# A GpSimd wait for landed rows in the middle of each attention step of a graph network kernel

## The reference

```
scores = einsum('ehd,ehd->eh', q[dst], k[src] + ep[:, None, :]) * scale
scores = scores * ew[:, None]
ex     = exp(scores - m[dst])              # m: maximum over the edges of a node
attn   = ex / segment_sum(ex, dst)[dst]
out    = segment_sum(attn[:, :, None] * v[src], dst)
x = x + alpha * (out @ Wo + bo);  x = x + beta * (gelu(norm(x) @ W1 + b1) @ W2 + b2)
```

## Time and profile before

| | |
|---|---|
| time, median of 3 runs | 2524.44 us (2523.85 to 2524.78) |
| span of the profiled execution | 2736.8 us |
| the profiled execution's own time | none is recorded beside its span |
| share of the span: PE, PEld, DVE, ACT, POOL | 77%, 59%, 80%, 56%, 59% |
| mean granted TensorE clock | 0.882 |
| indirect gathers of `kv_e` (L1358) | 752, of 953 ns mean on GpSimd |
| edge lists (L1337) | 94 |

### The profile page before, as it was taken

One profiled execution on the slowest core, in us unless ns is written; L12 is line 12 of the kernel. 1 busy time (PEld: TensorE's weight loads), 2 busy tenths in 40 slices (PEclk: granted clock), 3 DMA queues, 4 the chain that ended last, 5 costly groups with the idle time before them and its releaser, 6 DMA issues. The chain is left out here.

```text
span 2736.8 us, 41806 instructions
## 1 busy us (share of the span) xinstructions
PE 2107.6 (77%) x9647; PEld 1611.0 (59%) x9647; DVE 2183.1 (80%) x3415; ACT 1524.3 (56%) x4291; POOL 1618.3 (59%) x1808
## 2 busy tenths in 40 slices
PE   3999999999999999679815666666566666656666
PEld 2787878777777777533314455455455545545555
DVE  6888888888888888645546878878888788878793
ACT  5787888788877887433223444444444444444443
POOL 5666666666666666342246666666666666666642
PEclk8999999999999999889957788878878878887787
DMA  6232222222222222769856666666666666666651
GB/s 203 72 84 81 83 83 83 83 82 84 83 83 81 84 82 84 167 165 253 234 181 168 168 173 175 173 165 173 177 169 175 169 172 176 167 175 170 173 141 45
DMA packets 157414, 379.08 MB, mean 139 GB/s; under 512 B 47810, under 2 KB 63298, under 8 KB 157186
## 3 DMA queue, kind: packets, MB, share of 16 engines
q0 software_dynamic: 100544, 309.00, 40.6%
q1 hardware_dynamic: 44946, 68.53, 8.7%
q10 hardware_dynamic: 11904, 1.34, 0.4%
HBM read 353.36 MB, written 37.07 MB: 143 GB/s over the span
## 5 line engine op out<-in xcount | busy, mean ns | idle before, releaser
L1358 POOL DMA_INDIRECT kv_e<-kv_rows,edge x752 | 716.9, 953 | 408.4 <-issue 223.4
L487 POOL DMA_INDIRECT feat<-in_x_rows,idx x664 | 677.1, 1020 | 236.2 <-issue 234.8
L523 ACT ACTIVATE vsh<-feat,rec_a 128x256 f32<-128x256 f32 x1980 | 806.8, 495 | 8.9 <-DMA feat<-in_x_rows,idx 4.8
L1541 PE MATMUL ps_sum<-kv_e,ident 128*128 128x264 f32 x1504 | 473.8, 477 | 376.9 <-issue 264.2
L1541 PEld LDWEIGHTS ps_sum<-kv_e,ident 128*128 128x128 f32 x1504 | 352.5, 240 | 481.8 <-issue 283.6
L571 PE MATMUL ps_a<-msg,hot 128*128 128x257 f32 x1312 | 409.4, 393 | 4.0 <-issue 4.0
L573 PE MATMUL ps_a<-msg,hot 128*128 128x256 f32 x1312 | 390.6, 379 | 0.1
L575 PE MATMUL ps_a<-msg,hot 128*128 128x192 f32 x1312 | 320.2, 325 | 0.0
L573 PEld LDWEIGHTS ps_a<-msg,hot 128*128 128x128 f32 x1312 | 248.6, 190 | 38.2 <-issue 1.9
L575 PEld LDWEIGHTS ps_a<-msg,hot 128*128 128x128 f32 x1312 | 248.8, 190 | 34.9
L571 PEld LDWEIGHTS ps_a<-msg,hot 128*128 128x128 f32 x1312 | 222.2, 189 | 66.3 <-issue 66.3
(11 more groups left out here) (419 smaller groups left out, 3182.2 us busy)
## 6 DMA issues: line engine op xcount, KB each, us to landing
ef<-in_ef_t SPq DMA_DIRECT2D x84, 256.0 KB
kv_e<-kv_rows,edge POOLq DMA_INDIRECT x752
rows_e<-rows SPq DMA_DIRECT2D x41, 272.0 KB
feat<-in_x_rows,idx POOLq DMA_INDIRECT x664
rows_e<-in_ef_t SPq DMA_DIRECT2D x1, 7446.0 KB, 26.6
kv_rows<-kv SPq DMA_DIRECT2D x20, 260.0 KB, 2.5
rows_e<-in_ef_t SPq DMA_DIRECT2D x1, 3706.0 KB
x<-x_rows SPq DMA_DIRECT2D x23, 128.0 KB
```

Source lines behind the costliest of these rows:

```text
L487: pool.indirect_dma_start(out=feat[:, u, c, 0, :, :].rearrange("p a b -> p (a b)"), out_offset=None, in_=g.x_rows, in_offset=bass.Indirect ...
L523: ins = act.activation(vsh[:, u % TURN, c, j, :, :], feat[:, u % TURN, c, 0, :, :], ACT.Copy, scale=rec_a[:, u % 2, c, 1 + j:2 + j])
L1358: pool.indirect_dma_start(out=kv[:, u, s, :], out_offset=None, in_=g.kv_rows, in_offset=bass.IndirectOffsetOnAxis(ap=edge[:, u, s, DH + 1: ...
L1541: mm = pe.matmul(out, g.ident[:], kv[:, u, s, D:], start=(s == 0), stop=False, skip_group_check=True)
```

## The change

In the middle of a step, ahead of the edge list of the next step, GpSimd waits until four gathers of this step have landed. `v_kv[u]` has 128 for each of the t rounds before and 16 for each gather of this one, so `t * 128 + 64` is reached when the step's four gathers so far are all in. A semaphore that nobody waits for is raised then. The wait is in all 94 steps, those of the tail too; what is gathered, its order and its buffers stay the same.

```
                 for s in range(SLOTS):
                     if s == SLOTS // 2:
+                        pool.wait_ge(v_kv[u], t * (16 * SLOTS) + 16 * HALF)
+                        pool.sem_inc(v_asked_pool, 1)
                         if more:
                             pool.wait_ge(v_at, k + 2)
                             pool.wait_ge(v_read, k + 1)
```

## The result

| | before | after |
|---|---|---|
| time, median | 2524.14 us (2522.99 to 2524.78, 4 runs) | 2847.9 us (2844.3 to 2848.52, 4 runs) |
| span of the profiled execution | 2736.8 us | 2845.8 us, its own time 2847.47 |
| ratio | | 1.1281, 95% interval 1.1267 to 1.1294 |

Now and then an execution takes over 1.5% longer than the fastest of its kernel (3232.85 us in one case, where most took 2752 to 2768), and medians and ratios in this document are of the others alone.

The account below looks back on a forecast made before the run. The prediction took GpSimd's nine issues a step, 11.33 us, to bound the attention stage, with DVE right behind. Adding 3.4 us for each of 94 waits gave 2524.4 + 319.6 = 2844 us, range 2740 to 2885.

Parts of the forecast that it names:

- The price of the wait: GpSimd's mid-step gap grows from 0.30 us by landing plus restart, adding 3.34 to 3.54 us a step, taken as 3.4.
- landing to DVE's start: From the end of a step's last gather issue to DVE, which waits for it, starting: 2.95 to 2.99 us.
- GpSimd's restart beyond DVE's: Where both engines are let go together, GpSimd's next issue comes 0.67 to 0.87 us behind DVE.
- The 3.0 us made from the Trainium skill's fit: Alternative addition per mid-step wait: 2.6 us for one DMA, plus restart 0.67 less 0.30; total 2806 us.
- The beat as the bound: In the attention stage GpSimd's nine issues, 11.33 us a step, set the pace; the wait makes it 14.73.
- What is covered: The delayed edge list stays hidden behind four gathers, 5.0 us against 3.00 of landing; the added increment costs nothing.
- rival E: TensorE, its clock kept at 1.2 GHz by longer pauses, bounds the attention stage: 2938 us, chance 0.03.
- The step that was right for a wrong reason: Attention-stage stops of up to 12 us were taken as the profiled execution's, mostly absent from timed runs.
- the 2484.7 us worked out for a stage without them: End of the attention stage if GpSimd never waited, 198.7 us earlier than profiled.
- Rival A: Attention-stage stops occur in timed runs too, hiding 2.3 us of each wait: 120.9 us added, 2645 us, chance 0.11.
- The stretch outside the stage: Of the 212.4 us between profiled span and median, the attention stage without waits explained 198.7, within 14 us.
- The span forecast for the profile of after: Profiled span of the changed kernel: 2858 us, with the attention stage ending 120.9 us later than in the first profile.

Follow-up runs that it names:

- the three shorter waits: Kernel before plus a mid-step wait for three gathers, or for two, or for four behind the edge list's issue: 2728.97, 2610.87, 2725.96 us.
- the wait that is already met: Kernel before plus a mid-step wait for the step's edge list, already waited for, with the increment: 2521.82 us, ratio 1.000.
- with seven gathers: Kernel before with SP loading the eighth slot: ratio 0.9672; adding the change's wait 0.9985, or a wait for two gathers 0.9701.
- both waits: Kernel before plus the change's mid-step wait and a wait for all eight gathers at each step's end: 3208.4 us, ratio 1.1622.
- the wait at the end of the step: Kernel before plus a wait for all eight gathers at each step's end, none in the middle: 2878.62 us, ratio 1.0427.
- one wait a lap: Kernel before plus the change's wait in one step of each lap of four: u = 3 2770.62 us, u = 1 2786.02 us.

## Why the prediction was right

*The price of the wait.* Put at 3.34 to 3.54 us, taken as 3.4; measured 323.8 / 94 = 3.44. Both terms, read from engines that waited for something else, held as they were defined: landing to DVE's start 2.95 to 2.99 predicted, 2.91 in the row of after; GpSimd's restart beyond DVE's 0.67 to 0.87 predicted, 0.83 there. By the landings' own updates the same gap is 2.77 and 0.98. The 3.0 us made from the Trainium skill's fit ("DMA: Bandwidth & Descriptors", anatomy of one DMA on the gpsimd path) would have given 2806. Here the measurement decides for the rows.

*The beat as the bound.* Held: 94 times the price lies on top, and the three shorter waits follow it to within 3 us. The sum, 2844, is 3.9 us below the 2847.9 measured.

*What is covered.* Held: the edge list may be late (the wait behind it costs the same as the wait for three gathers), the increment is free (the wait that is already met). Once GpSimd has slack, a wait shorter than the slack is nearly free: with seven gathers, 7 us for 88.8, on a chip where about half of that slack came from the stops (an estimate, above).

*TensorE at its lower level (rival E).* Did not happen: at a clock of 0.78 TensorE was busy 836.84 of 1393 us, and even at a beat above 18 us, with both waits, the second cost what one wait costs.

*The step that was right for a wrong reason.* "I take these as stops that the profiled execution has and the timed ones mostly have not." The timed runs of the result indeed have none, and the 2484.7 us worked out for a stage without them is what this rested on. But they are no mark of a single profiled execution: on three chips out of four in the experiments the timed runs are long too, and the profiled execution of after, on the other side, agrees with its own time to 2 us. The first profile must have come from such a chip, or been taken in the same way; that is inferred from its stops and from the semaphore updates that it lacks, since no time stands beside it. Rival A, "the stops are real in the timed runs too", is thereby the other kind of chip: its price of 120.9 us agrees with what the wait at the end of the step costs there, 119.6. Had the result been timed on such a chip, the ratio would by this have been near 1.04 instead of 1.13, with a time near the 2879 of the wait at the end; that is an estimate, and it was not run. So the price of the wait was foreseen by its mechanism, and its base, a timed program without stops, was worked out. But that the changed kernel would meet the same kind of chip was not argued, since the prediction did not know of two kinds; there it was lucky.

*The stretch outside the stage.* The prediction left 13.7 us of the 212.4 without a place. The profile of the already met wait finds it. Against the first profile of before it is 217.1 us shorter (2519.7 for 2736.8): 195.9 in the stage, where the prediction had 198.7, 13.5 ahead of it (first gather at 1387.59 for 1401.05) and 7.8 behind it (45.6 us for 53.4). The span forecast for the profile of after, 2858, started from that first profile and is 12 us too long, mostly for the same reason: in the 2845.8 measured, the first gather is issued at 1389.94.

Open: why the engines stand on some chips and not on others, whether recording has a part in it, and why they move when the traffic is over. A full wait in every step removes the stops (none in the profiles with the wait at the end, with both, and with seven gathers and the change's wait); a wait for two of seven gathers in every step does not, nor does one wait a lap. I have no run that separates the gathers' traffic from the work of the engines around them.

## What to carry to other kernels

A wait for one's own DMA costs landing plus the issuing engine's restart, less the issues that run in between, here 2.8 + 1.0 - 0.3 us; their sum can be read before the change from other engines' rows. Each issue moved ahead of the wait takes its own length off the price, and a wait as short as the slack is free, so count the slack of the issuing engine first. And where a profile's span and the timed median differ by 8%, don't explain the difference away: sum the engines' own beats, see which of the two they give, and treat the other as a second case with its own price.

## What the runs showed of the hardware

The same program took 2522 us on one chip and 2746, 2759 and 2763 on three others, each figure steady within a per cent. Between the profiles of 2519.7 and 2760.9 us all of the difference lies in one stage but some 22 us (12.6 ahead of it, 8.9 behind it). In the second one DVE stands for "remote" for up to 13.7 us, 29 times and 186.8 us in all in 1220 us of the stage. At the stop that was looked at closely TensorE is recorded in drips, with the parts of one matmul 2.8 us apart, ScalarE stands for 10.1 us with no release shown, and a semaphore update of TensorE comes 12.6 us behind the recorded end of its matmul. The traces of the slow chips hold less than two thirds of the semaphore updates that the others hold, and what is cause and what effect is open. And GpSimd, held by a semaphore, needs 0.98 us from the last update of the landing to its next indirect DMA, where DVE needs 0.11.
